# Attention's row sums: inverted in compact form instead of after their spread; clamps and shifts of the score rows dealt out anew over three engines

## The reference

```
scores = relu(q @ k.T) * R_hat            # R_hat depends on the distance of the two positions
scores = where(above the diagonal, -inf, scores)
attn   = softmax(scores / sqrt(16))
ctx    = attn @ val ;  x = x + ga * (ctx @ Wo + bo)
```

## Time and profile before

| | PE (TensorE) | DVE (VectorE) | ACT (ScalarE) | POOL (GpSimd) |
|---|---|---|---|---|
| busy us | 1471.9 | 1203.2 | 1014.2 | 931.5 |
| share of the span | 83% | 68% | 57% | 52% |

### The profile page before, as it was taken

One profiled execution on the slowest core, in us unless ns is written; L12 is line 12 of the kernel. 1 busy time (PEld: TensorE's weight loads), 2 busy tenths in 40 slices (PEclk: granted clock), 3 DMA queues, 4 the chain that ended last, 5 costly groups with the idle time before them and its releaser, 6 DMA issues. The chain is left out here.

```text
span 1775.2 us, 43017 instructions
## 1 busy us (share of the span) xinstructions
PE 1471.9 (83%) x16126; PEld 1123.0 (63%) x16126; DVE 1203.2 (68%) x3588; ACT 1014.2 (57%) x1780; POOL 931.5 (52%) x1460
## 2 busy tenths in 40 slices
PE   6968999999999999999999999999523414989987
PEld 3534777777777777777777777777422304566565
DVE  7626787778778777877877787787897783222121
ACT  3435778777877877777787777877222300211211
POOL 3324766766675676667567667756442301223322
PEclk9987999999999999999999999999766655999999
DMA  6332221122122122222212211320521140234431
GB/s 204 128 127 93 84 67 57 58 87 62 54 84 67 56 68 78 73 91 85 65 56 72 76 60 54 86 66 24 177 106 48 59 128 23 73 79 99 120 79 23
DMA packets 81898, 141.89 MB, mean 80 GB/s; under 512 B 9904, under 2 KB 61504, under 8 KB 77600
## 3 DMA queue, kind: packets, MB, share of 16 engines
q1 hardware_dynamic: 74000, 128.23, 23.0%
q0 software_dynamic: 6464, 9.29, 3.0%
q10 hardware_dynamic: 1232, 1.71, 0.3%
HBM read 109.30 MB, written 29.89 MB: 78 GB/s over the span
## 5 line engine op out<-in xcount | busy, mean ns | idle before, releaser
L705 PE MATMUL score_ps<-region_s 128*128 128x512 bf16 (+3 forms) x1280 | 431.9, 354 | 32.7 <-DVE maxima L784 28.6
L751 ACT ACTIVATE region_p<-turn_ps 128x512 f32<-128x512 f32 x512 | 303.6, 602 | 174.9 <-PE turn_ps L716 169.7
L751 ACT ACTIVATE region_o<-turn_ps 128x512 f32<-128x512 f32 x576 | 339.7, 601 | 76.9 <-PE turn_ps L716 69.8
L716 PE MATMUL turn_ps<-ident,region_a 128*128 128x128 f32 x2048 | 342.3, 274 | 0.0
L716 PE MATMUL turn_ps<-ident,region_x 128*128 128x128 f32 x2048 | 340.5, 274 | 0.0
L784 DVE CUSTOM_DVE_ANT_0 region_x<-score_ps,region_t,maxima 128x512 f32<-128x512 f32 (+1 forms) x416 | 278.8, 707 | 90.0 <-PE score_ps L705 88.7
L813 POOL TENSOR_SCALAR region_a<-region_a,maxima 128x1152 f32<-128x1152 f32 (+6 forms) x224 | 271.8, 1213 | 103.1 <-ACT region_a L758 90.3
L716 PEld LDWEIGHTS turn_ps<-ident,region_a 128*128 128x128 f32 x2048 | 261.8, 141 | 43.9 <-ACT region_o L751 11.3
L716 PEld LDWEIGHTS turn_ps<-ident,region_x 128*128 128x128 f32 x2048 | 259.8, 142 | 28.9 <-issue 0.5
L784 DVE CUSTOM_DVE_ANT_0 region_a<-score_ps,region_t,maxima 128x512 f32<-128x512 f32 (+1 forms) x352 | 236.7, 699 | 29.5 <-PE score_ps L705 23.8
L784 DVE CUSTOM_DVE_ANT_0 region_a<-score_ps,region_t 128x384 f32<-128x384 f32 (+2 forms) x256 | 139.1, 553 | 86.8 <-PE score_ps L705 86.6
(11 more groups left out here) (197 smaller groups left out, 2053.5 us busy)
## 6 DMA issues: line engine op xcount, KB each, us to landing
region_t<-factor_rows SPq DMA_DIRECT2D x32, 1024.0 KB
region_x<-in_fc_t SPq DMA_DIRECT2D x16, 1024.0 KB, 8.2
region_s<-q_split SPq DMA_DIRECT2D x64, 192.0 KB
region_s<-k_split SPq DMA_DIRECT2D x64, 192.0 KB
region_x<-in_x SPq DMA_DIRECT2D x8, 1024.0 KB, 9.7
q_split<-region_o SPq DMA_DIRECT2D x16, 384.0 KB, 2.7
k_split<-region_t SPq DMA_DIRECT2D x16, 384.0 KB, 2.6
heads_out<-region_o SPq DMA_DIRECT2D x256, 17.0 KB
```

Source lines behind the costliest of these rows:

```text
L705: nc.tensor.matmul(score_ps[:, j % SB, 0:(hi - lo) * P], stacks[:, b, 0, t * P:(t + 1) * P], stacks[:, b, 1, lo * P:hi * P], start=True, s ...
L716: last = nc.tensor.transpose(turn_ps[:, (h * NR + j) % TB, q * P:(q + 1) * P], rows[t][:, k * P:(k + 1) * P], ident[:, :])
L751: nc.scalar.activation(weight(j), turn_ps[:, (h * NR + j) % TB, :], ACT.Exp).then_inc(exp_done, 1)
```

## The change

The reciprocal of the sums moves. After both dumps of a half-head have landed, SP gathers its 2048 sums from DRAM into a compact tile of 128x16 (`gather_sums`), VectorE inverts that tile, SP writes it back to a DRAM tensor `inverse` (`spread_inverse`), and what is later loaded with each value on 16 rows is already inverted (`load_inverse`). `normalise` has only the product left. The new steps have order values of their own: for batch 0 compact 39.4, invert 42.3, spread 43.3; for batch 1 34 more (8 to 9 rounds into the next head). The last half-head's three steps are in the mixture, the reciprocal at the end of its first loop turn. The loads of finished heads follow the spread step of head 8, and those of the last head follow its first spread step.

The second part: `ON_DVE` becomes tiles 15, 3, 2, 1, 0, 11, 7, 6 (14 goes; 11, 7 and 6 come), and `RELU_ON_ACT` becomes 14, 13, 10, 9. GpSimd now does both steps of 12, 8, 5 and 4.

```diff
+        def gather_sums(sp, h, b):
+            for i in range(2):
+                sp.wait_ge(dumped[i], DUMPED * (B * h + b + 1))
+            src = heads_out[h, HD:HD + 1, b * N:(b + 1) * N].rearrange("o (p t) -> p (o t)", p=P)
+            sp.dma_start(compact[:, b, :], src).then_inc(compacted[b], 16)
+
+        def spread_inverse(sp, h, b):
+            sp.wait_ge(inverted, h * B + b + 1)
+            dst = inverse[h:h + 1, b * N:(b + 1) * N].rearrange("o (p t) -> p (o t)", p=P)
+            sp.dma_start(dst, compact[:, b, :]).then_inc(spread[b], 16)
+
+        def load_inverse(sp, g, k):
+            src = inverse[k * (H // KC):(k + 1) * (H // KC), g * GW:(g + 1) * GW]
             src = bass.AP(tensor=src.tensor, offset=src.offset, ap=[src.ap[0], [0, HD], src.ap[1]])
+            sp.dma_start(inverse_of[g][:, k * GW:(k + 1) * GW], src).then_inc(ld_heads[g], 16)
...
-        def normalise(nc, dve, g, inverted):
-            done = g % (NG // B) + 1
+        def normalise(nc, dve, g):
             dve.wait_ge(ld_heads[g], HEADS_LOADS)
-            nc.vector.reciprocal(sums_of[g], sums_of[g]).then_inc(inverted, 1)
-            dve.wait_ge(inverted, done)
             both = context[:, g, :, :].rearrange("p k t -> p (k t)")
-            nc.vector.tensor_tensor(both, both, sums_of[g], ALU.mult).then_inc(ctx_normed, 1)
+            nc.vector.tensor_tensor(both, both, inverse_of[g], ALU.mult).then_inc(ctx_normed, 1)
...
-    ON_DVE = (15, 14, 3, 2, 1, 0)
-    RELU_ON_ACT = (13, 12, 11, 10, 9)
+    ON_DVE = (15, 3, 2, 1, 0, 11, 7, 6)
+    RELU_ON_ACT = (14, 13, 10, 9)
...
+    gathered_at = [NR // B * (b + 1) - 1 + PV_LAG + 4 for b in range(B)]
+    events += [(gathered_at[b] + 0.1, "compact", b) for b in range(B)]
+    events += [(gathered_at[b] + 3, "invert", b) for b in range(B)]
+    events += [(gathered_at[b] + 4, "spread", b) for b in range(B)]
...
+                elif what == "compact" and (h, j) != (H - 1, B - 1):
+                    if h:
+                        sp.wait_ge(spread[j], 16 * h)
+                    gather_sums(sp, h, j)
+                elif what == "spread" and (h, j) != (H - 1, B - 1):
+                    spread_inverse(sp, h, j)
+                    if (h, j) == (H // KC, 0):
+
+                        for g in range(NG):
+                            load_heads(sp, g, 0)
+                    if (h, j) == (H - 1, 0):
+
+                        sp.wait_ge(scaled, h * NS + (FREE_SCALED + last_of[0] + 1))
+                        for g in range(NG // B):
+                            load_heads(sp, g, 1)
+                        sp.wait_ge(spread[j], 16 * H)
+                        for g in range(NG // B):
+                            for k in range(KC):
+                                load_inverse(sp, g, k)
...
+                elif what == "invert" and (h, j) != (H - 1, B - 1):
+                    dve.wait_ge(compacted[j], 16 * (h + 1))
+                    nc.vector.reciprocal(compact[:, j, :], compact[:, j, :]).then_inc(inverted, 1)
...
+            gather_sums(sp, H - 1, B - 1)
             for g in range(GB, G):
                 load_heads(sp, g, 1)
+            spread_inverse(sp, H - 1, B - 1)
+            sp.wait_ge(spread[1], 16 * H)
+            for g in range(GB, G):
                 for k in range(KC):
-                    load_sums(sp, g, k)
+                    load_inverse(sp, g, k)
...
+                if s == 0:
+                    dve.wait_ge(compacted[B - 1], 16 * H)
+                    nc.vector.reciprocal(compact[:, B - 1, :], compact[:, B - 1, :]).then_inc(inverted, 1)
                 if GB <= s + 1 < G:
-                    normalise(nc, dve, s + 1, inverted)
+                    normalise(nc, dve, s + 1)
```

More of the change, by code:

```diff
@@ L70, in adaln_block @@
         heads_out = dram("heads_out", (H, HD + 1, TOK), F32)
+        inverse = dram("inverse", (H, TOK), F32)
         region_x = sb("region_x", [P, NT * D])
@@ L108, in adaln_block @@
         loaded = [ctx.enter_context(nc.semaphore("loaded0")), ctx.enter_context(nc.semaphore("loaded1"))]
+        compacted = [ctx.enter_context(nc.semaphore("compacted0")), ctx.enter_context(nc.semaphore("compacted1"))]
+        inverted = ctx.enter_context(nc.semaphore("inverted"))
+        compact = sb("compact", [P, B, BT])
+        spread = [ctx.enter_context(nc.semaphore("spread0")), ctx.enter_context(nc.semaphore("spread1"))]
         dumped = [ctx.enter_context(nc.semaphore("dumped0")), ctx.enter_context(nc.semaphore("dumped1"))]
@@ L112, in adaln_block @@
         ld_x2 = [ctx.enter_context(nc.semaphore(f"ld_x2_{i}")) for i in range(4)]
-        sums_of = [region_t[:, 0:1024], region_t[:, 1024:2048], region_s[:, 0:1024], region_s[:, 1024:2048]]
-        sums_of += [region_a[:, g * 1024:(g + 1) * 1024] for g in range(NG // B, NG)]
+        inverse_of = [region_t[:, 0:1024], region_t[:, 1024:2048], region_s[:, 0:1024], region_s[:, 1024:2048]]
+        inverse_of += [region_a[:, g * 1024:(g + 1) * 1024] for g in range(NG // B, NG)]
         def load_heads(sp, g, k):
@@ L119, in load_heads @@
             sp.dma_start(context[:, g, k, :], src).then_inc(ld_heads[g], 16)
-        def load_sums(sp, g, k):
-            src = heads_out[k * (H // KC):(k + 1) * (H // KC), HD, g * GW:(g + 1) * GW]
+        def gather_sums(sp, h, b):
[9 more added lines that the diff above has]
+            src = inverse[k * (H // KC):(k + 1) * (H // KC), g * GW:(g + 1) * GW]
             src = bass.AP(tensor=src.tensor, offset=src.offset, ap=[src.ap[0], [0, HD], src.ap[1]])
-            sp.dma_start(sums_of[g][:, k * GW:(k + 1) * GW], src).then_inc(ld_heads[g], 16)
+            sp.dma_start(inverse_of[g][:, k * GW:(k + 1) * GW], src).then_inc(ld_heads[g], 16)
         def load_x2(sp, x, i):
@@ L519, in attention @@
     x, vals, ident, heads_out = o["x"], o["vals"], o["ident"], o["heads_out"]
-    dumped, load_heads, load_sums, load_x2, normalise = (o[k] for k in ("dumped", "load_heads", "load_sums", "load_x2", "normalise"))
-    DUMPED = o["DUMPED"]
+    dumped, load_heads, load_inverse, load_x2, normalise = (o[k] for k in ("dumped", "load_heads", "load_inverse", "load_x2", "normalise"))
+    DUMPED, spread, compacted, inverted, compact, gather_sums, spread_inverse = (o[k] for k in (
+        "DUMPED", "spread", "compacted", "inverted", "compact", "gather_sums", "spread_inverse"))
     stacks, factors, vblock, loaded, load_head = (o[k] for k in ("stacks", "factors", "vblock", "loaded", "load_head"))
@@ L633, in attention @@
         turned, exp_done, pv_done, pv_saved = sem("turned"), sem("exp_done"), sem("pv_done"), sem("pv_saved")
-        inverted = sem("inverted")
         values_done = [sem("values_done0"), sem("values_done1")]
@@ L794, in _ @@
             for g in range(NG // B):
-                normalise(nc, dve, g, inverted)
+                normalise(nc, dve, g)
         @block.gpsimd
@@ L836, in mixture @@
     same_expert, rows_before, tile_of, row_of = g_("same_expert", "rows_before", "tile_of", "row_of")
-    dumped, load_heads, load_sums, load_x2, normalise = g_("dumped", "load_heads", "load_sums", "load_x2", "normalise")
-    DUMPED = o["DUMPED"]
+    dumped, load_heads, load_inverse, load_x2, normalise = g_("dumped", "load_heads", "load_inverse", "load_x2", "normalise")
+    DUMPED, spread, compacted, inverted, compact, gather_sums, spread_inverse = (o[k] for k in (
+        "DUMPED", "spread", "compacted", "inverted", "compact", "gather_sums", "spread_inverse"))
     ld_x, ctx_normed, region_c = g_("ld_x2", "ctx_normed", "region_c")
@@ L853, in mixture @@
         sem = lambda name: st.enter_context(nc.semaphore(name))
-        xb_done, proj_done, inverted = sem("xb_done"), sem("proj_done"), sem("inverted2")
+        xb_done, proj_done = sem("xb_done"), sem("proj_done")
         x2_done, rstd1_done, z_done, h2_done, rstd2_done = sem("x2_done"), sem("rstd1_done"), sem("z_done"), sem("h2_done"), sem("rstd2_done")
@@ L944, in _ @@
             load_x2(sp, x, 3)
-            for i in range(2):
-                sp.wait_ge(dumped[i], DUMPED * B * H)
+            gather_sums(sp, H - 1, B - 1)
             for g in range(GB, G):
                 load_heads(sp, g, 1)
+            spread_inverse(sp, H - 1, B - 1)
+            sp.wait_ge(spread[1], 16 * H)
+            for g in range(GB, G):
                 for k in range(KC):
-                    load_sums(sp, g, k)
+                    load_inverse(sp, g, k)
             for g in range(G):
```

## The result

The changed kernel takes 1834.12 us (median of 4 runs, 1832.64 to 1835.43) against 1777.76 us before (4 runs): ratio 1.0315, 95% interval 1.0302 to 1.0328, slower by 56 us. The forecast was 1860 with its own range from 1834 to 1891. The sign and the mechanism are as forecast; the size is not. The profiled execution took 1835.43 us, its span 1833.4.

A forecast was written before the change was run, and what follows sets the result against it. Attention was taken as bound by TensorE, the stage behind it by VectorE. 1777.0 + 114 (loop) + 3 (head 8) - 7.5 (end of attention) - 26 (next stage) = 1860 us; own range 1834 to 1891, overall 1803 to 1898.

The forecast's parts named there:

- The loop: In attention, load, dumps, gather, reciprocal, scores, next load take 38.2 us a half-head against 34.43; 30 turns, +114 us.
- VectorE's catching up: In attention, behind the reciprocal, eight score pieces (4.6 us) and three shifts (2.2) come before SP's next load.
- the first term: In each half-head of attention, from SP's load until the dumps have landed and the gather may begin: 28.7 us.
- the 3 us of head 8: Head 8's eight loads of finished heads, behind the reciprocal and before the next load, cost 3 us once.
- Clamps and shifts: Their new division in attention: counted as nothing under the loop; without its cover -0.4 us a half-head, -12 us.
- case A: In attention the sums land under 27 us after the load, no loop forms: 1731 us; chance 0.14.
- The end of attention: SP, no longer VectorE's four large reciprocals, ends attention, at about 1268.5 instead of 1276: -7.5 us.
- The next stage: Behind attention, the last four token groups each lose a 6.47 us reciprocal from the chain: -26 us.
- The signs named: In attention, load distance near 38 us, VectorE waits 4 to 6 us, score matmuls waiting over 100 us in all.
- B: In attention the loop forms but is short, score banks swallowing most of the wait: +60, 1803 us; chance 0.09.
- C: The gather in attention is as slow as the cold small load: +6.7 us a turn, 1945 us; chance 0.07.
- D: In attention VectorE's small shifts and GpSimd's tile 14 shift block each other: at most 61 us, 1792 us; chance 0.02.

The follow-up runs named there:

- the faster version: The first experiment's kernel with head 8's loads back behind its first dumps, tile 14's shift back on VectorE, small tiles wholly on GpSimd: 1705.8 us.
- the first experiment's kernel: The changed kernel with the reciprocal 9 rounds and the store of the inverses 12 rounds later, except in the last head: 1727.31 us.

## Why the prediction was right in kind and 26 us too high

*The loop: right, and its terms.* Gather at 28.7 us after the load: measured 28.8 in the half-head shown. Gather and semaphore 2.3 + 0.1: measured 1.59 (1144.38 to 1145.97). Here the row chosen was the wrong one: the small index moves (1.9 us) were called the lower bound, and the gather was quicker still, 1.54 to 1.79 us from its issue to the start of the reciprocal in the 31 half-heads; that is below the 2.2 of the sum and the 2.0 that the prediction gives beside it. Reciprocal, eight pieces, three shifts and SP's step 0.24 + 6.8 + 0.05 = 7.1: measured 6.75. Together the turn is 1.1 us shorter than forecast in the half-head shown; over all but head 8's it is 37.3 on average, +2.8 instead of +3.8. Its 29 distances give (37.27 - 34.43) x 29 = +82, head 8's another 4.9 (forecast 3), the first load's 2.5 us and 2.4 us behind the last load complete the +92 (forecast +117). Why the first load comes 2.5 us later is open; in the other kernels it stands between 176.5 and 180.5, with either dealing. The mis-sized terms of the sum are the gather and VectorE's catching up, in the mean of the 28 turns 1.64 for 2.4 and 6.75 for 7.1, with the first term at 28.9 for 28.7; the step itself held, and three runs that each changed one part of the loop moved the distance of the loads with it.

*A reason that did not hold.* The dumps land late "because SP's load stands before them in the same queue", the prediction says. With 15/16 of that load's 1 MB part left out the gather still came 26.6 us after the load: the length of the first term was read rightly from the rows, but its reason holds, as far as this run tests it, for only 2.5 of the 29 us. The rest is when the data is saved (21.5 us after the load) and how long the dumps need.

*Slips in the sums.* The range leaves out the 3 us of head 8 that the forecast has; with them it starts at 1837, and 1834.12 lies just under it. That the measured time lies at the end of the range, and not outside it, is luck. The eight pieces come to 4.66 us by the rows, taken as 4.6, and the shorter tail is 27.8 where the bounds use 27.9. Tile 12's shift was GpSimd's before as well, so GpSimd gets its clamp alone.

*Clamps and shifts: zero under the loop, right; the value without its cover, wrong.* The text said -0.4 us a half-head and the dealing alone measured -0.82 (34.43 to 33.61). By the matmuls' waits the text was right: 59.3 / 29 = 2.04 us went, and 48.0 / 29 = 1.66 came in their place. But TensorE's weight loads are held longer than the matmuls behind them. Their waits from 200 to 1200 us, in the kernel before and in the one with the dealing alone:

```profile
PEld score_ps L705 <- DVE maxima L784: 55.1, 147, 0.8
...
PEld pv_ps L731 <- ACT region_o L751: 26.3, 29, 0.9
PEld pv_ps L731 <- ACT region_p L751: 23.1, 29, 0.8
PEld turn_ps L716 <- ACT region_o L751: 10.2, 29, 0.4
PEld turn_ps L716 <- ACT region_p L751: 7.2, 29, 0.3
```

```profile
PEld turn_ps L716 <- POOL region_x L821: 55.1, 29, 1.9
...
PEld score_ps L705 <- DVE maxima L784: 29.1, 148, 0.2
...
PEld pv_ps L731 <- ACT region_o L751: 8.9, 30, 0.3
```

Gone are (55.1 - 29.1 + 26.3 - 8.9 + 23.1 + 10.2 + 7.2) / 29 = 2.9 us a half-head, and 55.1 / 29 = 1.9 came, a gain of 1.0 against the measured 0.82; the matmuls' waits gave 0.4. So the size was read from the wrong queue of TensorE. This is a sum after the fact, and no run tests it. With -0.82 for -0.4 case A (1731) would have been 1717; with the wait away it measured 1727, and 7 of these 10 us are head 8's half-head, which took 40.4 us there.

*The end of attention* -7.5: measured -7.35. *The next stage* -26: measured -27.2, groups 15 to 16 us apart.

*The signs named.* The VectorE wait of 4 to 6 us: 4.2. The distance near 38: 37.3. Exponential waits gone, no large reciprocals: so. "Over 100 us" of TensorE's score matmuls waiting: wrong, 76.2; the loss shows more fully in these matmuls' weight loads, 132.5 us. The mask wait of 51.2 us is no part of what the loop costs: with the wait for the sums taken away it is 51.4.

*The rivals.* A needs sums within 27 us of the load; they came 30 us and more after it. B (a turn costing 2 us, 1803) is 31 us under the measured 1834, hardly farther off than the forecast above it; but its mechanism, score banks that swallow most of the wait, is not there, since the 6.75 us behind the reciprocal are the same in each turn. C is out: no gather was near 5.1 us. D's mechanism is real, its price was not: the engines do hold each other off, for some 1.2 us in each half-head, and getting 0.65 of that back changed nothing. That is so for tile 2's shift; in the run with the short load the same effect on tile 11's shift stood inside the loop and made the turn longer.

## What to carry to other kernels

When a change puts a wait for a DMA into the order of an engine that works strictly in order, follow from the end of that wait to the next issue of the transfer it depends on: if that closes a loop, its length is the new period, everything queued between the wait and that issue counts, and the same wait a few instructions later may be free. A good edit (here the dealing, -26 us, and the compact sums, -30 us) can be hidden completely by the place of one small instruction, so it pays to try each part alone and each new wait at a second place. An instruction whose duration grows with what runs beside it is a wait in disguise, and what it costs depends on whether it stands on the path.

## What the runs showed of the hardware

VectorE's shifts from and to on-chip memory and GpSimd's instructions exclude each other for a whole instruction: 414 ns became 1645 ns beside GpSimd's shift of 1.91 us, and the end of the one hung on the end of the other at two different starts. In the faster version two of GpSimd's masks, issued while VectorE's shift still ran, took 1.25 us, where two in the first experiment's kernel (at 1144.06) took 0.65 us. VectorE's score pieces, which read the matmul banks, kept their 0.75 us beside GpSimd's shifts. The Trainium skill, "SBUF — State Buffer", section "Who interferes with whom", says that VectorE in a two-port mode and GpSimd take a shared pair of ports by turns, the second blocking fully; the timelines here agree, for the shifts; that VectorE's shift runs in such a mode is not shown by any run. It also says that the order of issue decides who blocks; the two cases shown, one each way, agree.

A gather of 2048 values in 128 rows of 64 bytes took 1.54 to 1.79 us from its issue to the start of the instruction that waited for it, over 31 half-heads; the smallest transfers of the kernel before have a median of 1.9 us to landing.
